# Attention and expert layer on one core: the chains of the second layer norm, the stores of its rows, and the tables of the slot map

## The reference

```python
x = x + xattn(layernorm(x), ctx)          # 16 heads of 16, softmax over 64 keys
h = layernorm(x)                          # the second layer norm
shared = (silu(h @ sh_gate.T) * (h @ sh_up.T)) @ sh_down.T
probs  = softmax(h @ gate_w.T)            # (4096, 8)
w, idx = top_k(probs, 2); w = w / w.sum(-1)
routed = sum_k w[k] * expert[idx[k]](h)   # the same SwiGLU with 8 sets of weights
x = x + shared + routed
```

## Time and profile before

| | |
|---|---|
| median of 3 runs | 737.58 us (736.78 to 748.9) |
| the profiled execution, its own time | 740.04 us |
| its span | 738.2 us |
| mean clock of TensorE | 0.907 |
| TensorE busy | 619.7 us (84% of the span) |
| VectorE busy | 449.1 us (61%) |
| ScalarE busy | 346.3 us (47%) |
| GpSimd busy | 394.8 us (53%) |

### The profile page before, as it was taken

One profiled execution on the slowest core, in us unless ns is written; L12 is line 12 of the kernel. 1 busy time (PEld: TensorE's weight loads), 2 busy tenths in 40 slices (PEclk: granted clock), 3 DMA queues, 4 the chain that ended last, 5 costly groups with the idle time before them and its releaser, 6 DMA issues. The chain is left out here.

```text
span 738.2 us, 15686 instructions
## 1 busy us (share of the span) xinstructions
PE 619.7 (84%) x5294; PEld 418.2 (57%) x5294; DVE 449.1 (61%) x1041; ACT 346.3 (47%) x561; POOL 394.8 (53%) x325
## 2 busy tenths in 40 slices
PE   4688668999964869778869899999999999999991
PEld 2243224565643535445435568787788777878780
DVE  5958896577785545798996645454445444454540
ACT  3796636777855746354213434333333333233330
POOL 6579686778773101223203446647665665666543
PEclk9898985687867969999999999999999999999996
DMA  8500000222214076955301655547665655566643
GB/s 260 164 2 1 0 1 2 44 40 41 39 30 130 1 188 170 242 170 150 93 1 54 176 109 88 100 75 105 88 98 94 105 94 97 94 103 98 86 58 36
DMA packets 103820, 65.09 MB, mean 88 GB/s; under 512 B 78594, under 2 KB 96964, under 8 KB 103748
## 3 DMA queue, kind: packets, MB, share of 16 engines
q1 hardware_dynamic: 88916, 40.86, 23.2%
q0 software_dynamic: 14832, 23.24, 18.7%
HBM read 29.47 MB, written 17.96 MB: 64 GB/s over the span
## 5 line engine op out<-in xcount | busy, mean ns | idle before, releaser
L1393 PE MATMUL bank<-arena 128*128 128x34 f16 (+6 forms) x1284 | 136.5, 250 | 36.7 <-DVE bank L1007 8.2
L1393 PE MATMUL bank<-qx,arena 128*128 128x256 f16 (+1 forms) x1584 | 158.1, 290 | 2.8 <-ACT hidden L784 2.6
L663 POOL DMA_INDIRECT out<-w_stage,map_i x71 | 113.7, 1601 | 73.0 <-DMA out<-w_stage,map_i 37.3
L1393 PEld LDWEIGHTS bank<-qx,arena 128*128 (+1 forms) x1584 | 127.0, 102 | 25.2 <-issue 9.7
L1393 PEld LDWEIGHTS bank<-arena 128*128 128x128 f16 (+2 forms) x1284 | 73.3, 107 | 87.2 <-issue 47.0
L650 POOL DMA_INDIRECT qx<-rows_d,map_i x71 | 72.3, 1018 | 92.9 <-DVE map_i L1273 40.2
L1362 DVE TENSOR_TENSOR hidden<-bank,hidden 128x512 f32<-128x512 f32 x71 | 49.1, 691 | 112.5 <-ACT hidden L891 88.3
L1393 PE MATMUL bank<-arena,w_stage 128*128 x852 | 104.7, 273 | 2.0 <-ACT w_stage L897 0.9
L891 ACT ACTIVATE hidden<-bank 128x512 f32<-128x512 f32 x71 | 42.4, 597 | 135.6 <-PE bank L1393 111.5
L1393 PE MATMUL bank<-qx,w_sh 128*128 128x512 f16 x384 | 95.6, 402 | 3.7 <-ACT qx L842 3.7
L1393 PE MATMUL bank<-arena,qx 128*128 (+1 forms) x316 | 84.1, 388 | 14.9 <-DVE arena L954 12.4
(11 more groups left out here) (183 smaller groups left out, 754.3 us busy)
## 6 DMA issues: line engine op xcount, KB each, us to landing
w_stage<-in_w_all SPq DMA_DIRECT2D x27, 512.0 KB, 4.7
x_sb<-in_x SPq DMA_DIRECT2D x8, 512.0 KB, 8.2
rows_d<-arena SPq DMA_DIRECT2D x8, 512.0 KB, 3.5
out<-x_sb POOLq DMA_DIRECT2D x8, 512.0 KB
qx<-rows_d,map_i POOLq DMA_INDIRECT x71
qx<-qx SPq DMA_TRANSPOSE x71
out<-w_stage,map_i POOLq DMA_INDIRECT x71
arena<-arena SPq DMA_TRANSPOSE x32, 2.5
```

The costliest lines, as they stand in the source:

```text
L663: pool.indirect_dma_start(out=out, out_offset=bass.IndirectOffsetOnAxis(ap=map_i[:, 1, i:i + 1], axis=0), in_=y_sb[:, r], in_offset=None, ...
L1393: return pe.matmul(o, a, b, start=first, stop=last, skip_group_check=not check)
```

## The change

1. `rsqrt` becomes `rsqrt_guess` (three instructions) and `rsqrt_round` (three per round). The iterate lies in a PSUM bank (bank 6 for the first layer norm, bank 7 for the second), and each round's first two instructions change their order, so that a link of the rounds has one input in PSUM and at most one in SBUF. The last round writes the result to SBUF.
2. The first chain of the second norm moves from unit 15, where it stood ahead of `rows_of(10)`, to unit 16, behind `normalise(14)`. VectorE runs a unit more (`run_units(unit, 4)`), so that `rows_of(14)` is in the attention and only `rows_of(15)` in step 0. The second chain is split: guess and first round in step 1, the rest in step 2. Gates 0 and 1 wait for it.
3. TensorE: `project(14)` and `project(15)` move in front, `transpose_x2(0)` waits no longer for the weights, and weight 2 is waited for in `down(0)`.
4. SP: stores of x2 are issued as soon as their rows are ready, 0 and 1 ahead of all transposes, the others right behind their own group's transposes. The weight loads 7 and 8 go behind stores 5 and 6, the rest behind store 7.
5. One weight is split per step in steps 9 to 22 (`SPLITS_IN`), `GATE_STEP` is later for groups 4 and 6, and the router is one step later from `weights` on.
6. `one_hot` builds a table of 16 picks with three instructions over broadcast operands, all in float16.

```diff
@@
-        lane_val = sb("lane_val", [P, PC], F32)
+        lane_val = sb("lane_val", [P, PC], F16)
...
-        pick_tile = carve([PICKS], F32)
-        pick_lane = carve([PICKS], F32)
+        pick_tile = carve([PICKS], F16)
+        pick_lane = carve([PICKS], F16)
@@
-        GATE_STEP = (3, 3, 4, 5, 6, 8, 9, 10)
+        GATE_STEP = (3, 3, 4, 5, 7, 8, 10, 10)
...
-        SPLITS_IN = (0, 0, 2, 0, 0, 2, 0, 0, 2, 1, 1, 1, 1, 1, 1, 1, 1, 1, 1, 1, 0, 0, 0, 0, 0, 0,
-                     1, 1, 1, 1, 1, 2)
-        N_EARLY, LATE_STEP = 17, 26
+        SPLITS_IN = (0, 0, 1, 0, 0, 1, 0, 0, 1, 1, 1, 1, 1, 1, 1, 1, 1, 1, 1, 1, 1, 1, 1, 0, 0, 0, 0,
+                     1, 1, 1, 2, 2)
+        N_EARLY, LATE_STEP = 17, 27
@@
-        def rsqrt(dve, link, var, ve, bit, t, y):
+        def rsqrt_guess(dve, link, var, ve, bit, y):
 
             link(dve.tensor_scalar(ve, var, EPS, None, ALU.add))
             link(dve.tensor_scalar(bit, ve.bitcast(I32), 1, None, ALU.logical_shift_right))
             link(dve.tensor_scalar(y.bitcast(I32), bit, -1.0, MAGIC, ALU.mult, ALU.add))
-            for _ in range(3):
-                link(dve.scalar_tensor_tensor(out=t, in0=y, scalar=-0.5, in1=y, op0=ALU.mult, op1=ALU.mult))
-                link(dve.tensor_tensor(t, t, ve, ALU.mult))
-                link(dve.scalar_tensor_tensor(out=y, in0=t, scalar=1.5, in1=y, op0=ALU.add, op1=ALU.mult))
+
+        def rsqrt_round(dve, link, ve, t, y, out):
+
+            link(dve.scalar_tensor_tensor(out=t, in0=ve, scalar=-0.5, in1=y, op0=ALU.mult, op1=ALU.mult))
+            link(dve.tensor_tensor(t, t, y, ALU.mult))
+            link(dve.scalar_tensor_tensor(out=out, in0=t, scalar=1.5, in1=y, op0=ALU.add, op1=ALU.mult))
@@
             def store_x2(g):
+                sp.wait_ge(x2l_ready, g + 1)
                 sp.dma_start(rows_t[:, bass.ts(g, GT), 0:C],
...
+            store_x2(0)
+            store_x2(1)
             for g in range(2, NG):
                 transpose_x2(g)
-                store_x2(g - 2)
-                load_w(g + 5)
-            store_x2(NG - 2)
-            store_x2(NG - 1)
-            for q in range(NG + 5, 3 * (E + 1)):
+                store_x2(g)
+                if g >= 5 and g < NG - 1:
+                    load_w(g + 2)
+            for q in range(9, 3 * (E + 1)):
@@
-                if u == NU - 1:
-                    scale_and_shift2(slice(0, LN2_FIRST * GT))
                 if known(u, 5):
                     rows_of(u - 5)
                 if known(u, 2):
                     normalise(u - 2)
                 if u == NU:
-                    split_lo(0)
+                    scale_guess2(slice(0, LN2_FIRST * GT))
+                    scale_and_shift2(slice(0, LN2_FIRST * GT))
                 if u == NU + 1:
                     low_half(0)
+                    split_lo(0)
                 if u == NU + 2:
+                    low_half(1)
                     split_lo(2)
-                    low_half(1)
@@
-                for j in range(PC):
-                    k = PC * c + j
-                    dve.tensor_scalar(hot_tile[:, c % 2, j], slot_iota[:, :], pick_tile[:, k:k + 1],
-                                      lane_val[:, j:j + 1], ALU.is_equal, ALU.mult)
-                    ins = dve.tensor_scalar(hot_lane[:, c % 2, j], lane_iota[:, :], pick_lane[:, k:k + 1],
-                                            None, ALU.is_equal)
-                ins.then_inc(hot_ready, 1)
+                at = slice(PC * c, PC * (c + 1))
+                link3(dve.tensor_tensor(hot_tile[:, c % 2], slot_iota[:, :].unsqueeze(1).to_broadcast([P, PC, NS]),
+                                        pick_tile[:, at].unsqueeze(2).to_broadcast([P, PC, NS]), ALU.is_equal))
+                dve.tensor_tensor(hot_lane[:, c % 2], lane_iota[:, :].unsqueeze(1).to_broadcast([P, PC, P]),
+                                  pick_lane[:, at].unsqueeze(2).to_broadcast([P, PC, P]), ALU.is_equal)
+                dve.tensor_tensor(hot_tile[:, c % 2], hot_tile[:, c % 2],
+                                  lane_val[:, :].unsqueeze(2).to_broadcast([P, PC, NS]),
+                                  ALU.mult).then_inc(hot_ready, 1)
@@
                 if k == 0:
-                    rows_of(NU - 2)
+                    rows_of(NU - 1)
                 if k == 1:
-                    rows_of(NU - 1)
+                    scale_guess2(slice(LN2_FIRST * GT, NT))
+                if k == 2:
                     scale_and_shift2(slice(LN2_FIRST * GT, NT))
...
-            run_units(unit, 3)
+            run_units(unit, 4)
@@
                 if g < 2:
                     pe.wait_ge(y_added, NU)
+                    pe.wait_ge(rstd_ready, 2)
@@
                 if k == 0:
                     pe.wait_ge(of_ready, NU)
+                    pe.wait_ge(w_lo[2], 1)
@@
-            for r in range(3):
+            project(NU - 2)
+            transpose_x2(0)
+            for r in range(2):
                 pe.wait_ge(w_lo[r], 1)
-            transpose_x2(0)
             for k in range(FS):
                 up(k)
                 if k == 0:
                     transpose_x2(1)
-                if k < 2:
-                    project(NU - 2 + k)
+                    project(NU - 1)
```

41 lines of the change are left out of this document (24 added, 17 removed).

## The result

730.62 us median (725.01 to 733.26, 11 runs) against 739.17 (736.66 to 748.9, 11 runs) for the kernel before on the same chip: ratio 0.987, 95% interval 0.984 to 0.991. The change gains 1.3% where 3.3% were forecast; the time lies above the range. The profiled execution has a span of 728.6 us, 9.6 less than before.

What follows compares the result with a forecast made beforehand. Bounds: an attention-end chain, engine and queue waits up to step 11, VectorE's router arithmetic, then TensorE in the constant expert slots. Summed span 231.0 + 64.5 + 72.0 + 25.4 + 320.0 = 712.9 us; forecast 713, range 704 to 727.

Steps and rivals of the forecast that it cites:

- term 3: Router on VectorE, product of step 11 to last one-hot table: 74.8 us would become 72.0, -2.8 us.
- Term 1: End of the attention, up to up(0): its start would move from 237.1 to 231.0 us, -6.1 us.
- Rival B: End of the attention held by the transposes of o, its gain about zero: 719 us, chance 0.09.
- Term 2: Shared network, up(0) to VectorE's product of step 11: 75.1 us would become 64.5, -10.6 us.
- (c): Up(0) to product 11: early stores end ScalarE's 5.09 us wait; gate 2 waits 3.3 us for logits instead of 6.5, -3.2.
- (a): Up(0) to product 11: project(15) goes ahead of up(1), where TensorE waits for ScalarE's copy anyway, -1.3 us.
- (b): Up(0) to product 11: gates 0 and 1 wait 1.3 us for the split norm chain instead of 2.7 for cast halves, -1.4.
- (d): Up(0) to product 11: gate 7's rows land at 58.8 us, about 4.5 us of DMA wait remain, -0.3 us.
- (e): Up(0) to product 11: fewer stops raise TensorE's clock, its work taking 55 us instead of 59.5, -4.4 us.
- Rival A: Up(0) to product 11: crowded transfers delay the last three transposes and a landing, +7, 720 us, chance 0.20.
- Term 4: Last one-hot table to product of step 31: 5.9 us to product 26, then steps of 3.90; 25.4 us, -5.8.
- rivals C and D: One-hot tables: several 16-bit elements at once, 706 or 704 us, chance 0.07; or stepped-output price, 781 us, chance 0.03.

Runs made afterwards that it cites:

- e9: Kernel of e8 plus VectorE taking each gate's logits in the gate's own step, routing choice beginning in step 11 again: 717.4 us median.
- e12: Changed kernel with SP's stores of the rows back in their old places, each two groups behind its transposes: 734.1 us, ratio 0.990.
- e10: Kernel of e9 with the chains of the first layer norm in SBUF as before the change: 716.0 us median.
- e6: Changed kernel with residual and statistics of unit 13 ahead of the split of weight 0 on VectorE: 721.6 us median.
- e2: Changed kernel with the output product of unit 14 moved behind up(0) and the second transposes: 726.4 us, ratio 0.980.
- e5: Changed kernel with gate 7 one step later, in step 11, and best_first moved to step 12: 721.1 us, ratio 0.974.
- e17: Changed kernel with 22 unused products of 128x512 issued after up 10, ahead of gates 6 and 7: 728.1 us, ratio 0.987.
- e18: Kernel of e9 with SP's stores of groups 5, 6 and 7 behind the last transposes, not between them: 709.5 us, ratio 0.961.
- e3: Changed kernel with one-hot tables built by 32 small instructions per 16 picks, from 32-bit picks, as before: 735.8 us, ratio 0.992.
- e4: Changed kernel with the odd weight splits 9 to 19 moved from GpSimd to VectorE: 725.8 us, ratio 0.979.
- e7: Kernel before the change, with only the stores of each group moved right behind its transposes: 731.5 us, ratio 0.987.
- e15: Kernel of e9 measured again, unchanged, on the same chip as e14: 713.9 us median.
- e14: Kernel of e8 measured again, unchanged, on the same chip as e15: 721.4 us median.
- e13: Changed kernel with gate 6's 16 small products issued 18 times over before gate 7: 727.6 us, ratio 0.983.
- e8: Changed kernel with product 14 behind up(0), gate 7 in step 11 and odd splits 9 to 19 on VectorE: 717.1 us, ratio 0.966.

## Why the prediction was wrong

It failed by 15.7 us in the stretches, in no single place, and the time lies above the range. Only term 3 had the wrong sign; every other term was too large.

**The front, taken as unchanged: 3.9 us.** The first of unit 0's clips starts 2.2 us later than before (104.2 and 102.0). The stretch 80:100, before and after:

```profile
80.00:100.00 20.00, 11.96 (x84) 5.74 (x88) 19.19 (x28) 10.06 (x20) 14.53 (x11) 1.00 0.00 1
```

```profile
80.00:100.00 20.00, 12.69 (x59) 5.49 (x59) 16.87 (x25) 8.63 (x16) 14.54 (x10) 0.83 0.00 1
```

TensorE was granted 0.83 of its full clock, not 1.00, and got through 59 products in place of 84. The front's code being the same, those clips start anywhere from 101.0 (e9) to 109.1 us (e12). The PSUM chains are not the reason (the pairs under e10). The clock up to the last clip was 0.78 here, 0.82 before and 0.84 in the earliest; that it falls by chance is argued, and why it falls is open. The forecast had no term for that scatter, nor for the rest, from 316.8 to 325.6 us.

**Term 1, 2.7 us short.** project(13) came 4.3 us earlier relative to the clips, 3.9 forecast. Behind it the sum took 1.5 us for each project; at the low clock they took 2.74 and 2.20. And it had the residual 1.6 us "behind a split of VectorE": that split took 2.18 us, held by GpSimd, so TensorE waited 2.91. e6 and e2 show that this queue, not the low halves or copies, set up(0). Rival B had the right place for the loss but another engine.

**Term 2, 3.7 us short.** (c) held: 3.4 us of logits against 3.3 forecast. (a) held. (b) gave 0.6 of 1.4: 2.1 us are left before gates 0 and 1. (d) failed by 1.2: gate 7 could start 60.4 us after up(0), not 58.8, and waited 5.4. (e) failed by 1.9: TensorE's busy time fell by 4.0, but 1.5 of it is the project that (a) counted, so the clock gave back 2.5 of 4.4. The forecast averaged the clock and didn't ask where it falls. It falls in three places: 0.53 in 256.0:259.6 behind gates 0 and 1, 0.51 in 266.3:269.8 behind gate 2, and 0.51 in 297.0:303.9 at gate 7, half of the whole; e5, e17 and e18 take out the last. Rival A, the crowded transfers, is not borne out in the changed kernel: the issues of the last three groups took 5.13, 5.72 and 6.53 us, before 5.13, 6.16 and 7.09, and gate 7 ran 1.3 us behind the last one in both. The stores in SP's queue hold gate 7 only where other waits are gone (e18).

**Terms 3 and 4, 6.2 us short together (-2.4 of -8.6).** The tables held, 4.82 us a chunk against 4.8 and 4.6 in sum (e3), so rivals C and D are out, and E with links of 0.18 us. Two parts of term 3 failed. The first is "one more on GpSimd ... +1.2". These rows of VectorE and the 4.10 us shown above are the five long ones:

```profile
311.38 2.02 DVE L1294 TENSOR_TENSOR hidden<-hidden 128x512 f16<-128x512 f32 x1
...
319.83 1.93 DVE L1177 TENSOR_TENSOR w<-m 128x32 f32<-128x32 f32 x1
...
339.48 2.02 DVE L1217 SCALAR_TENSOR_TENSOR limit_e<-big_e,before_e 128x8 f32<-128x8 f32 x1
...
353.52 2.01 DVE L1294 TENSOR_TENSOR hidden<-hidden 128x512 f16<-128x512 f32 x1
```

Without a GpSimd split beside them they take 0.68, 0.40, 0.17, 0.68 and 2.29 us: 7.9 us too much. A sixth is a short one:

```profile
332.61 1.25 DVE L1196 COPY before_e<-arena 128x7 f32<-128x7 f32 x1
```

It takes 0.17 us in e4, so 9.0 us in all. The kernel before had such rows as well, three low halves (L1280) of 2.02 us, one of 1.03 and the same copy, 5.5 us in all. So six GpSimd splits in place of five cost 3.5 us more where the sum had 1.2: what a split costs hangs on the instructions that meet it. e4 recovers 4.3 us net of the splits that it adds.

The second is "the idle 1.04 and 1.97 us go: -3.0". VectorE still stands 0.58, 0.25 and 1.04 us for ScalarE (at 324.67, 326.21 and 330.56), so 1.1 us was won. With two splits more on VectorE (+2.4), one product and low half more (+1.4) and the tables (-4.4) these make the measured +1.8.

Term 4 had the product of step 26 right, 6.0 us behind the last table against 5.9. But the steps to 27 and to 31 took 4.9 and 4.3 us, not 3.90: TensorE waited 0.84 us for VectorE's addition L1349, and L1071 took 2.48 us at 407.06 beside a GpSimd split.

That the stores would end ScalarE's wait was right. In the kernel before it paid as much as the tables (3.8 to 4.5 us in e7, 4.6 in e3); what it pays within the change is open (e12). Each term was taken at what the change makes possible, the waits behind it at their length in a kernel without the change, and so all the errors went one way.

## What to carry to other kernels

Ask of a wait in an in-order queue what stands behind it that somebody else needs: three stores (e18 against e9, 3.8 us), the logit reductions (e15 against e14, 4.8) and one residual (e6, 2.4), moved by a place or a step, were together worth more than the rewritten tables (e3, 4.6). Where VectorE bounds a stretch, count GpSimd's instructions beside it as VectorE's own time, since what it blocks shows only as a long row, not as an idle one. And a gain in one stage must be read from that stage, against a profile whose steps ahead of it ran alike: the front and the routed part scattered by more than most of these edits gave.

## What the runs showed of the hardware that I had not expected

- A VectorE instruction with two SBUF inputs that meets a GpSimd one waits until its very end, at any size: 0.17 us became 2.02 (L1217, eight elements), 2.29 became 4.10. Two with one input did so too: the copy L1196 (0.17 us became 1.25, to 333.86, where GpSimd's split ended at 333.84) and the shift L429 (1.09 us, to 222.01, where GpSimd's subtraction ended at 221.97).
- Behind 304 products of 16 columns in 8.1 us with a gap of 0.42 us, TensorE's down and up took 2.72 and 3.43 us, the lower clock (1.2 GHz, 0.50 granted in 294.0:300.8) for at least a part of them (e13); behind 22 products of 512 columns and two gates in their place they took 1.47 and 2.75, full clock (e17). The length of a wait alone doesn't tell which it will be: before gate 7 the clock stayed up behind 1.83 us (e5) and 2.71 us (e10) and fell behind 2.77 (e8) and 3.35 (e9), but it also fell behind the 2.1 us before gates 0 and 1 (0.53 in 256.0:259.6 of the changed kernel).
- 160 such small products took 4.16 us, 26 ns each, where 16 of them show as 0.55 us.
- The same code reached the same instruction 9.5 us apart (last clip, 207.7 in e9 and 217.2 us in e12), at a granted clock of 0.84 and 0.80 up to there.
